# Another order of work in the opening of the first FFN: low parts, high parts, identity products and the activation table

## The reference

```python
def _L0_ffn_ref(x, w_gate, w_up, w_down):
    h = jax.nn.silu(jnp.einsum('bsh,hi->bsi', x, w_gate)) * jnp.einsum('bsh,hi->bsi', x, w_up)
    h_sparse = _sparsify_2to4(h)          # of each four neighbours the two largest by magnitude stay
    return jnp.einsum('bsi,ih->bsh', h_sparse, w_down)
x = L0_attn_x                              # (2, 1024, 256); w_gate, w_up 256x1024; w_down 1024x256
x = x + 0.5 * _L0_ffn_ref(_layernorm(x, axis=-1), L0_ffn_w_gate, L0_ffn_w_up, L0_ffn_w_down)
x = x + _L0_attn_ref(_layernorm(x, axis=-1), ...)
x = x + 0.5 * _L0_ffn_ref(_layernorm(x, axis=-1), L0_ffn_w_gate, L0_ffn_w_up, L0_ffn_w_down)
```

## Time and profile before

| | us |
|---|---|
| median of 3 executions | 777.62 (776.43 to 778.4) |
| the profiled execution, own time | 777.72 |
| its span, first to last instruction | 776.0 |
| PE busy | 736.0 (95%) |
| DVE busy | 682.1 (88%) |
| ACT busy | 511.1 (66%) |
| POOL busy | 256.5 (33%) |

### The profile page before, as it was taken

How to read it: one execution, slowest core, us unless ns; L and a number is a source line. 1 busy time by engine, 2 the same in 40 slices (tenths; PEclk the granted TensorE clock), 3 DMA queues, 4 the chain that set the end, 5 groups by cost and what they waited for, 6 DMA issues and landing times.

```text
span 776.0 us, 15886 instructions
## 1 busy us (share of the span) xinstructions
PE 736.0 (95%) x5298; PEld 519.7 (67%) x5298; DVE 682.1 (88%) x1985; ACT 511.1 (66%) x1021; POOL 256.5 (33%) x360
## 2 busy tenths in 40 slices
PE   4999999989999999999999999999999999999997
PEld 3777888787776555555555555555555588888886
DVE  4889999988699999999999999999992569989897
ACT  6444444314325999999999999999998534443441
POOL 1133335117742222333222233265254103334330
PEclk9999999999999999999999999999999999999999
DMA  8000000006773123433223334423331000000001
GB/s 314 30 27 1 1 1 1 1 2 229 222 231 73 44 44 78 95 78 70 52 47 76 87 77 114 112 52 83 83 79 38 9 7 1 1 28 1 28 2 54
DMA packets 28017, 49.90 MB, mean 64 GB/s; under 512 B 4896, under 2 KB 13248, under 8 KB 27424
## 3 DMA queue, kind: packets, MB, share of 16 engines
q1 hardware_dynamic: 27872, 48.83, 24.4%
q10 hardware_dynamic: 64, 0.07, 0.0%
HBM read 20.35 MB, written 14.88 MB: 45 GB/s over the span
## 4 chain that ended last, share of the span: by engine, by line
PE 62%; DVE 23%; issue 6%; ACT 4%; POOL 3%; DMA 1%; PEldq 0%; DVEq 0%; PEld 0%; SPq 0%; POOLq 0%; ACTq 0%
PE att_o_ps L1528 18%; PE att_s_ps L1512 12%; PE att_m_ps L1471 11%; PE ffn_gate L218 6%; PE ffn_up L218 5%; PE ffn_y_ps L351 5%; DVE ffn_h L566 3%; DVE att_maxima L1601 3%; DVE ffn_hs L524 2%; DVE att_scratch L1598 2%; DVE ffn_rank L510 1%; DVE ffn_xn L181 1%; POOL qkv_turned L878 1%; DVE ffn_pair_max L498 1%; DVE ffn_pair_min L499 1%
## 5 line engine op out<-in xcount | busy, mean ns | idle before, releaser
L1651 ACT ACTIVATE att_probs<-att_s_ps 128x512 f32<-128x512 f32 x630 | 306.1, 573 | 22.5 <-PE att_s_ps L1512 17.8
L1598 DVE CUSTOM_DVE_ANT_0 att_scratch<-att_m_ps,att_causal 128x384 bf16<-128x384 f32 (+3 forms) x512 | 221.3, 486 | 7.9 <-PE att_m_ps L1471 7.0
L1471 PE MATMUL att_m_ps<-k,q 64*128 64x256 f32 (+3 forms) x768 | 205.1, 362 | 6.2 <-DVE att_maxima L1601 3.2
L1512 PE MATMUL att_s_ps<-q,k 64*128 64x512 f32 (+2 forms) x756 | 204.2, 379 | 1.5 <-ACT att_probs L1651 0.8
L1512 PEld LDWEIGHTS att_s_ps<-q,k 64*128 64x128 f32 x756 | 118.0, 185 | 67.6 <-ACT att_probs L1651 55.5
L1528 PE MATMUL att_o_ps<-att_probs,att_vs 128*32 128x512 f32 (+3 forms) x1536 | 158.1, 499 | 0.9 <-ACT att_sums L1672 0.7
L1471 PEld LDWEIGHTS att_m_ps<-k,q 64*128 64x128 f32 x768 | 120.7, 185 | 52.5 <-DVE att_maxima L1598 23.4
L454 ACT ACTIVATE ffn_a<-ffn_h 128x512 f32<-128x512 f32 x64 | 40.5, 633 | 110.8 <-DVE ffn_h L566 110.8
L1703 POOL TENSOR_SCALAR_AFFINE_SELECT att_probs<-att_probs 128x512 f32<-128x512 f32 x128 | 79.0, 635 | 103.3 <-ACT att_probs L1651 103.1
L630 POOL TENSOR_TENSOR ffn_hs_lo<-ffn_hs,ffn_hs_hi 128x512 fp32r<-128x512 f32 x48 | 77.4, 1635 | 106.2 <-ACT ffn_hs_hi L427 106.2
L1601 DVE TENSOR_REDUCE att_maxima<-att_m_ps 128x1 f32<-128x512 f32 x128 | 86.7, 687 | 8.1 <-PE att_m_ps L1471 6.7
(11 more groups left out here) (128 smaller groups left out, 1372.1 us busy)
## 6 DMA issues: line engine op xcount, KB each, us to landing
q_rows<-qkv_parts SPq DMA_DIRECT2D x16, 512.0 KB, 5.2
q<-q_rows SPq DMA_DIRECT2D x32, 256.0 KB, 4.5
q<-q SPq DMA_DIRECT2D x16, 512.0 KB, 4.3
k<-k_rows SPq DMA_DIRECT2D x16, 160.0 KB, 5.3
k_rows<-qkv_parts SPq DMA_DIRECT2D x8, 256.0 KB, 3.2
k<-k SPq DMA_DIRECT2D x16, 128.0 KB, 4.5
out_num<-att_sums SPq DMA_DIRECT2D x128, 16.0 KB
x<-in_x SPq DMA_DIRECT2D x1, 1536.0 KB, 11.4
```

Of the source, the lines that this page charges most:

```text
L1471: pe.matmul(m_ps[unit_bank(n)][:, COLUMNS[m]], q[g % 2][m_lane, t // TPC, h, t % TPC * P:(t % TPC + 1) * P], k[g % 2][m_lane, keys], start ...
L1512: last = pe.matmul(s_all[S_BANK["s", n]][:, at:at + w], k[g % 2][lane, kb * P:(kb + 1) * P], q[g % 2][lane, qc, h, q0:q0 + w], start=True, ...
L1598: dve.tensor_tensor_reduce(out=scratch[bank][:, at], in0=m_ps[bank][:, at], in1=causal[:, N - n:], scale=1.0, scalar=LOWEST, op0=ALU.add, ...
L1651: act.activation(probs[u % len(probs)][:, h, SPAN[u]], s_all[S_BANK["s", n]][:, SPAN[u]], ACT.Exp, scale=SCALE).then_inc(exp_done, 1)
```

## The change

In the first FFN alone (`first_loads`), and there in the opening:

- DVE normalises x right behind the statistics. The low part of the gate's piece 0 goes to POOL, in two instructions of 512 elements a partition, behind the inverse deviation of chunk 0. The low part of the up's piece 1 stays on DVE in two instructions, one ahead of and one behind `ffn_xt_lo`.
- PE no longer waits for both pieces before the first unit: `first_unit` waits for each part just before the matmul that reads it. The up matmuls of a unit come behind the gate's, as before.
- ACT makes the high parts of pieces 2 to 5 one at a time, each behind the SiLU of units 0 to 3.
- A SiLU of one column of the identity stands at the head of ACT's program.
- PE makes 24 products of the identity with itself, from the moment x of chunk 0 is there, into a bank that unit 1 overwrites.

```diff
+    def low_part_of(self, dve, n, k):
+        _, _, read, hi, lo = self.loads[n]
+        dve.wait_ge(self.hi_ready, n + 1)
+        dve.tensor_tensor(lo[:, k], read[:, k], hi[:, k].bitcast(F32), ALU.subtract).then_inc(self.ready, 1)
+
+    def first_low_parts(self, pool):
+        _, _, read, hi, lo = self.loads[0]
+        pool.wait_ge(self.hi_ready, 1)
+        for k in range(read.shape[1]):
+            pool.tensor_tensor(lo[:, k], read[:, k], hi[:, k].bitcast(F32), ALU.subtract).then_inc(self.gate_lo_ready, 1)
...
+        def first_unit():
+
+            for n, (w, ps) in enumerate(zip((wg, wu), gu[0])):
+                pe.wait_ge(w_loads.hi_ready, n + 1)
+                for k in range(KT):
+                    if w is wg:
+                        pe.wait_ge(normed.hi_ready, k + 1)
+                    pe.matmul(ps[:], w[0][:, k, 0, 0, :], normed.xt_hi[:, k, :], start=(k == 0), stop=False)
+                    pe.wait_ge(w_loads.gate_lo_ready if w is wg else w_loads.ready, k + 1)
+                    pe.matmul(ps[:], w[1][:, k, 0, 0, :], normed.xt_hi[:, k, :], start=False, stop=False)
+                    if w is wg:
+                        pe.wait_ge(normed.lo_ready, k + 1)
+                    last = pe.matmul(ps[:], w[0][:, k, 0, 0, :], normed.xt_lo[:, k, :], start=False, stop=(k == KT - 1))
+                last.then_inc(gate_done if w is wg else up_done, 1)
...
         if first_loads:
             pe.wait_ge(x_loads.ident_ready, 3)
+            pe.wait_ge(x_loaded[0], 16)
+            for _ in range(IDENTITIES):
+                pe.transpose(gu[1][1][:, :P], normed.ident[:], normed.ident[:])
         if not joined:
             normed.transpose(pe, 0)
-        if first_loads:
-            pe.wait_ge(w_loads.ready, 2)
...
                     act.activation(silu[:, j % 2, :], gu[j % 2][0][:], ACT.Silu).then_inc(silu_ready, 1)
+                if j in extra:
+                    w_loads.high_parts(act, extra[j])
...
         if first_loads:
+            act.wait_ge(x_loads.ident_ready, 2)
+            act.activation(silu[:, 1, :1], normed.ident[:, :1], ACT.Silu)
             w_loads.high_parts(act, 0)
             w_loads.high_parts(act, 1)
...
-        if first_loads:
-            for n in range(2, len(w_loads.loads)):
-                w_loads.high_parts(act, n)
-        stage(0, 0, sparse=False)
+        stage(0, 0, sparse=False, extra={0: 2, 1: 3, 2: 4, 3: 5} if first_loads else {})
...
             normed.statistics(dve, 0)
-            if first_loads:
-                w_loads.low_parts(dve, 0)
             normed.normalise(dve, 0)
             if first_loads:
-                w_loads.low_parts(dve, 1)
+                w_loads.low_part_of(dve, 1, 0)
             for k in range(KT):
                 normed.low_parts(dve, 0, k)
+            if first_loads:
+                w_loads.low_part_of(dve, 1, 1)
...
             normed.inverse_deviation(pool, 0)
+            if first_loads:
+                w_loads.first_low_parts(pool)
```

More of the change, by code:

```diff
@@ L235, in __init__ @@
         self.ready = ctx.enter_context(nc.semaphore(f"{tag}_w_ready"))
+        self.gate_lo_ready = ctx.enter_context(nc.semaphore(f"{tag}_w_gate_lo_ready"))
     def high_parts(self, act, n):
@@ L281, in ffn_programs @@
     LAST = (CHUNKS * BLKS - 1) * J
+    IDENTITIES = 24
     assert BLKS == 2 and CHUNKS >= 3
@@ L380, in last_down @@
                 pe.drain().then_inc(y_done, 1)
+        def first_unit():
[11 more added lines that the diff above has]
+                last.then_inc(gate_done if w is wg else up_done, 1)
         def stage(c, blk, hidden=True, multiply=True, first=False, more=True):
             for j in range(J):
+                if first and first_loads and j == 0:
+                    first_unit()
+                elif hidden:
+                    gate_up(c, blk, j, first)
                 if hidden:
-                    gate_up(c, blk, j, first)
                     if blk == 1 and j == 1 and more:
@@ L432, in last_high_part, with stage @@
             act.activation(hs_hi[:, BLKS - 1, j, cols], hs[:, j, cols], ACT.Copy).then_inc(hi_ready, 1)
-        def stage(c, blk, hidden=True, sparse=True, more=True):
+        def stage(c, blk, hidden=True, sparse=True, more=True, extra={}):
             for j in range(J):
```

## The result

| | before | after |
|---|---|---|
| median beside each other, 7 executions each | 777.58 (776.43 to 778.4) | 774.76 (771.46 to 777.42) |
| ratio | | 0.995, 95% interval 0.9932 to 0.9969 |
| the profiled execution: own time, span | 777.72, 776.0 | 772.42, 770.7 |

The change made the kernel 2.8 us faster by the first medians (forecast: 4.2).

The account below looks back on a forecast made before the run. The opening's chain of waits bounds it: ACT's work before the first SiLU, then DVE, later PE. 777.72 - 4.2 (some 2.6 from ACT, the rest from earlier products and faster PE) = 773.5, less 0.10: 773.4 us; range 771.9 to 776.2.

Parts of the forecast that it names:

- ACT: Opening: taking high parts and table load from ahead of the first SiLU gives some 2.6 us of the gain.
- S + 2.6: Opening: DVE's low part of piece 2 starts no earlier than 2.6 us after the first SiLU's start.
- W: Start of DVE's low part of piece 2, end of the opening: 18.0 us forecast against 22.18 before.
- The port: Opening: DVE's normalisation tiles and POOL's gate subtractions shut each other out; tiles 2 and 3 end at 12.6 us.
- D: Time of one strided POOL subtraction for the gate's low part: 1.7 us, range 1.29 to 2.44.
- Rival (a): Opening: normalisation gets through before POOL's subtractions; 5.2 us earlier, 772.4 us; chance 0.20.
- The first unit: Opening, unit 0: gate, up, SiLU and `h` times summed, putting piece 2's low part 4.2 us earlier, at 18.0.
- S: Start of ACT's first SiLU: forecast 15.4 us.
- H: Start of DVE's `h` of unit 0: forecast 16.8 us; piece 2's low part follows no earlier than 0.61 later.
- PE's clock: Opening: 24 identities raise PE to 2.4 GHz, so first-unit matmuls start 0.23 us apart instead of 0.43.
- Rival (b): Opening: identities fail to raise PE's clock, matmuls stay 0.43 us apart; 2.4 us earlier, 775.2 us; chance 0.27.
- None by a clock: After the opening: later work hangs on earlier work by semaphores, so the end comes earlier by as much as the opening.

## Why the prediction was right

By its own steps:

- **ACT.** Right in kind and size: 2.6 said, 2.64 measured with that part alone. The one-column SiLU and the table load lay in ACT's idle time. The condition S + 2.6 decided as said (15.23 + 2.55 = 17.78), and the high parts of pieces 3 to 5 stayed covered: from W to `h` of unit 4 it is 11.04 us, before 10.99.
- **The port.** Right: tile, subtraction, tile, subtraction, two tiles. D was 1.61 from start to start and 1.57 for the second, not 1.7; without stride 1.3. So the added 0.38 for the stride should have been 0.27, and the tiles ended at 12.1, not 12.6. The estimate of 2.0 by the page GPSIMD Engine Reference of the Trainium skill ("Performance pitfalls for Q7 kernels") was further off. Rival (a) did not happen. "Key points" of that page of the Trainium skill names contention with DVE instructions in a two-port mode or with two SBUF inputs, so a tile with one tensor input contends only in that mode. The tiles took 1.65 and 1.60, so they did contend; which mode they run in no run here shows, so the rule itself is not tested.
- **The first unit.** S 15.4 said, 15.23 measured; H 16.8 and 16.60; W 18.0 and 17.78. The sums agree better than their steps, which is partly luck: the tiles ended 0.5 earlier than said, and the way from there to PE's first gate product took 1.28 in place of 1.0. The two waits inside the unit did not happen. The low parts were ready at 14.54 and 15.52, and the gate's sixth matmul (14.80) and the up's fifth (15.95) came in PE's own rhythm.
- **What is not ACT's.** Of W's 4.40, 1.76 are left beside ACT's 2.64. Without identities only 0.31 of them remain (19.54 against 19.23), and PE's first gate product starts at 13.36 where it was 13.47. So the low parts' order, as the change has it, gives little by itself; nearly all of the rest needs the faster PE. The old order with ACT's part and the identities was not run.
- **PE's clock.** Right in the mechanism: without the identities W is 1.4 later. I had 1.8, since I let the clock rise at 18.9 as before; it rose at 17.5. That the 24 were enough was said with doubt, and no run varied their number. Rival (b) came in one of the experiments.
- **The end.** Here a step was too simple. "None by a clock" is true of semaphores and not of PE: the falls of its clock in later phases differ from execution to execution and move the end by some 3 us between a mean of 0.991 and one of 0.996. The opening gave 4.4 in all profiles of this kernel (4.25 to 4.4 in W and in C), the first medians 2.8, the pooled ones 3.8. The sum also held the 1.72 us between span and own time fixed, and with identities they are 1.98 in the mean of the changed kernel's 20 executions: 0.3 us of the gain go there. The rest of the 1.4 between 773.4 and 774.76 I put down to the clock; that is argued from the table by clock, not shown.
- **The range.** Its upper end has a slip: in (b) with D = 2.44 each D counts twice, so W is 21.3, a gain of 0.9 and not 1.4, and the end is 776.7 and not 776.2. The result lies inside either.

## What to carry to other kernels

Look for work that stands ahead of a latency-bound first result only by program order: moving ACT's bulk work behind the first SiLU gave more than half of the gain (2.64 of 4.40 at W, 2.39 of 4.36 at C). A second engine helps only where its instructions and those of the first don't take turns at the same port: POOL's subtraction was free beside DVE reading PSUM, and beside the normalisation it cost more than it brought. Filler work ahead of the first products can raise PE's clock, but count what it costs outside the span too, and that it failed in one profile of nine. Where a kernel's executions differ by several us, read a change of a few us at a mark in the profile, and compare executions of like granted clock, before believing a median of seven.

## What the runs showed of the hardware

- A normalisation tile of one tensor input and two pointer scalars waits for a POOL subtraction of two SBUF inputs (1.60 to 1.65 in place of 0.4); DVE instructions with one input in PSUM do not (`ffn_xt_lo` 1.30 for two beside POOL's 1.54).
- A stride of 16 bytes costs a 512-element subtraction 0.27 us on POOL (3.18 against 2.65 for two, start of the first to end of the second). With DVE idle the strided one takes 1.53, against 1.29 for one with contiguous inputs.
- PE's clock, raised by filler products, fell again before its real work in one profile, and in another kernel during a wait of 2.27 us. In the first PE had been busy 1.44 of 3.0 us, but it was busy 1.20 in two other profiles that kept the fast clock. The printed granted clock is 1.00 before the first rise, though matmuls are 0.43 us apart; after a fall it prints 0.50 at the same spacing.
- With the 24 identities an execution's own time is up to 3.49 us over its span (mean 2.06 of 74), without them never more than 1.78 (68 executions).
